# Joining a sequence's query-row transfers in the second attention of a two-layer kernel

## The reference

```
x = x + L0_attn(layernorm(x))          # linear attention, 16 heads of 8
x = x + L0_ffn(layernorm(x))           # 8 experts, each takes its top 129 tokens
x = x + L1_attn(layernorm(x))          # changed here
x = x + L1_ffn(layernorm(x))           # fft, product, inverse fft

def L1_attn(x):                        # x: 8 x 512 x 128, HEAD_D = 8, 16 heads
    qkv = x @ w_attn                   # 128 columns of q, 8 of k, 8 of v
    q = qkv[..., :D].reshape(Bv, Tv, H, HEAD_D).transpose(0, 2, 1, 3)
    k, v = qkv[..., D:D + HEAD_D], qkv[..., D + HEAD_D:]
    att = einsum('bhqd,bkd->bhqk', q, k) / sqrt(8), causal
    y = einsum('bhqk,bkd->bhqd', softmax(att), v)
    return y @ w_proj
```

## Time and profile before

| | us |
|---|---|
| median of three timed runs (lowest, highest) | 917.9 (916.76, 918.37) |
| the profiled execution's own time | 917.51 |
| its span, first to last instruction | 915.8 |
| start of the second attention's first query transfer | 442.60 |
| first scores of turn 0 | 500.40 |
| first scores of turn 1 | 548.09 |

### The profile page before, as it was taken

How to read it: one execution, slowest core, us unless ns; L and a number is a source line. 1 busy time by engine, 2 the same in 40 slices (tenths; PEclk the granted TensorE clock), 3 DMA queues, 4 the chain that set the end, 5 groups by cost and what they waited for, 6 DMA issues and landing times.

```text
span 915.8 us, 15035 instructions
## 1 busy us (share of the span) xinstructions
PE 689.0 (75%) x4377; PEld 413.0 (45%) x4409; DVE 578.8 (63%) x1934; ACT 336.8 (37%) x614; POOL 336.3 (37%) x438
## 2 busy tenths in 40 slices
PE   2788998860399999992553878888787878788866
PEld 1455665540178877771220324343433334243325
DVE  8388888869323344436474776858585868768126
ACT  1422322125032232320301646555455545455642
POOL 0475555610578667740000222222222222223324
PEclk9999999985599999995555999979898989989898
DMA  9100000005122222231011010101000000000003
GB/s 296 58 1 1 1 0 0 1 1 149 34 45 41 38 38 44 39 50 34 29 42 37 14 33 15 36 16 37 19 31 26 23 32 15 32 13 1 3 1 92
DMA packets 41861, 32.43 MB, mean 35 GB/s; under 512 B 5120, under 2 KB 38448, under 8 KB 41792
## 3 DMA queue, kind: packets, MB, share of 16 engines
q1 hardware_dynamic: 32608, 24.10, 8.5%
q0 software_dynamic: 7840, 6.86, 5.0%
q10 hardware_dynamic: 1344, 0.62, 0.3%
HBM read 13.60 MB, written 8.13 MB: 24 GB/s over the span
## 4 chain that ended last, share of the span: by engine, by line
PE 21%; DVE 13%; issue 9%; SPq 6%; ACT 2%; DMA 2%; POOL 1%; DVEq 0%; POOLq 0%; ACTq 0%
PE bank L1665 5%; PE wide L1652 5%; DVE masked L1321 5%; SPq L1543 5%; PE bank L1604 5%; PE bank L1677 2%; DMA qT<-mT 2%; ACT pexp L1475 2%; DVE mx L1321 2%; DVE st L286 1%; SPq L1549 1%; PE bank L1689 1%; PE bank L1579 1%; DVE q_rest L1279 1%; PE bank L1586 1%
## 5 line engine op out<-in xcount | busy, mean ns | idle before, releaser
L1321 DVE CUSTOM_DVE_ANT_0 masked<-bank,mask_qk 128x128 f32<-128x128 f32 (+2 forms) x496 | 216.6, 487 | 60.7 <-PE bank L1604 58.9
L1427 POOL TENSOR_SCALAR_AFFINE_SELECT pexp<-pexp 128x256 f32<-128x256 f32 x256 | 103.0, 407 | 363.6 <-ACT pexp L1475 360.6
L1475 ACT ACTIVATE pexp<-wide 128x1024 f32<-128x1024 f32 (+3 forms) x256 | 168.6, 707 | 161.8 <-PE wide L1652 161.0
L1604 PE MATMUL bank<-kTm,qT 128*128 128x128 bf16 (+3 forms) x474 | 117.0, 314 | 29.2 <-DVE mx L1321 23.8
L1652 PE MATMUL wide<-qT,kTe 128*128 128x256 bf16 (+3 forms) x503 | 113.3, 325 | 32.9 <-DMA qT<-mT 23.8
L1604 PEld LDWEIGHTS bank<-kTm,qT 128*128 128x128 bf16 x496 | 44.2, 101 | 129.9 <-DVE mx L1321 100.5
L1665 PE MATMUL bank<-pexp,vx 128*32 128x512 f32 (+3 forms) x1024 | 96.6, 450 | 2.2 <-POOL pexp L1427 1.1
L1068 ACT ACTIVATE hT<-wide,b1T 128x512 f32<-128x512 f32 x64 | 44.0, 688 | 137.0 <-PE wide L1088 137.0
L935 POOL DMA_INDIRECT x_row<-xln_dram,row_u x64 | 63.4, 990 | 52.8 <-DVE slot_tok L813 33.6
L1652 PEld LDWEIGHTS wide<-qT,kTe 128*128 128x128 bf16 x512 | 46.0, 102 | 76.2 <-ACT pexp L1475 27.1
L942 POOL DMA_INDIRECT x_dram<-yg,row_u x40 | 63.8, 1595 | 31.1 <-DVE yg L991 21.1
(11 more groups left out here) (226 smaller groups left out, 1039.8 us busy)
## 6 DMA issues: line engine op xcount, KB each, us to landing
qT<-qp SPq DMA_DIRECT2D x288, 32.0 KB
x_sb<-in_L_attn_x SPq DMA_DIRECT2D x8, 256.0 KB, 6.9
w_sb<-in_L_ffn_w SPq DMA_DIRECT2D x1, 2048.0 KB, 12.4
xln_dram<-rx SPq DMA_DIRECT2D x8, 256.0 KB, 2.3
out_x<-x_sb SPq DMA_DIRECT2D x8, 256.0 KB, 2.3
x_dram<-x_sb SPq DMA_DIRECT2D x5, 256.0 KB, 3.5
x_sb<-x_dram SPq DMA_DIRECT2D x5, 256.0 KB, 2.8
x_row<-xln_dram,row_u POOLq DMA_INDIRECT x64, 2.6
```

The costliest lines, as they stand in the source:

```text
L1321: ins = nc.vector.tensor_tensor_reduce(out=masked[:, n % 4, at], in0=bank_of(n)[:, at], in1=mask_qk[:, T - w:T], scale=1.0, scalar=LEAST, ...
L1427: nc.gpsimd.affine_select(out=pexp[:, n % 4, :, 0:P], in_=pexp[:, n % 4, :, 0:P], pattern=[[0, 2], [1, P]], compare_op=ALU.is_ge, fill=0.0 ...
L1475: nc.scalar.activation(pexp[:, n % 4, :, 0:w], psE[n % 2][:, :].rearrange("p (h t) -> p h t", h=2)[:, :, 0:w], ACT.Exp, scale=SCALE).then_ ...
L1604: ins = nc.tensor.matmul(place[:, hh * w:(hh + 1) * w], qT[:, b % 2, h + hh, k * P:(k + 1) * P], kTm[:, b % 2, 0:w], start=True, stop=True)
```

## The change

A sequence's query rows come in nine transfers of 128 KB, one for each pair of query part and key part: from all 128 partitions of `qp` into 8 partitions of `qT`, with all 16 heads. To that end `wq2` orders the columns as (feature, head). `qT` gets a third buffer (`QB = 3`), which lengthens the MEMSET of partitions 64 to 127 by half. The four semaphores of the quads become one, so each maximum waits for all nine transfers. SyncE issues sequence b + 2 whole in turn b, once the scores of sequence b - 1 are done. The shift rows are one transfer of 48 KB from 48 partitions into 3.

```
-        qT = sb("qT", [P, 2, HEADS, T], BF16)
+        qT = sb("qT", [P, QB, HEADS, T], BF16)
...
-        q_row = [Q(f"q_rows_of_quad_{qd}", PARTS * PARTS, 16) for qd in range(NQ)]
+        q_row = Q("q_rows", PARTS * PARTS, 16)
...
-        q_mTp, q_mT, q_mrow = Q("neg_max_T_psum"), Q("neg_max_T"), Q("shift_rows", PARTS, 16)
+        q_mTp, q_mT, q_mrow = Q("neg_max_T_psum"), Q("neg_max_T"), Q("shift_rows", 1, 16)
...
-            nc.vector.tensor_copy(wq2[:, :].rearrange("p (q l h) -> p q l h", l=L, h=4),
-                                  wa_sb[:, 0:D].rearrange("p (q h l) -> p q l h", h=4, l=L)).then_inc(q_init.sem, 1)
+            nc.vector.tensor_copy(wq2[:, :].rearrange("p (l h) -> p l h", l=L),
+                                  wa_sb[:, 0:D].rearrange("p (h l) -> p l h", l=L)).then_inc(q_init.sem, 1)
...
-            for qd in range(NQ):
-                act.wait_ge(q_row[qd].sem, q_row[qd].at(b, 0))
+            act.wait_ge(q_row.sem, q_row.at(b, 0))
...
-        def sp_q_rows(sp, b, quads):
-
-            for qd in quads:
-                if b >= 2:
-                    sp.wait_ge(q_sp.sem, q_sp.at(b - 2, 2 * NT * (qd + 1)))
-                for n in range(PARTS):
-                    sp.wait_ge(q_qpart.sem, q_qpart.at(b, 2 * n + 1))
-                    for j in range(PARTS):
-                        row = (n * PARTS + j) * L
-                        sp.dma_start(qT[row:row + L, b % 2, 4 * qd:4 * qd + 4, :],
-                                     qp[32 * qd:32 * qd + 32, n, :]).then_inc(q_row[qd].sem, 16)
+        def sp_q_rows(sp, b):
+
+            if b >= QB:
+                sp.wait_ge(q_sp.sem, q_sp.at(b - QB, NX))
+            for n in range(PARTS):
+                sp.wait_ge(q_qpart.sem, q_qpart.at(b, 2 * n + 1))
+                for j in range(PARTS):
+                    row = (n * PARTS + j) * L
+                    sp.dma_start(qT[row:row + L, b % QB, :, :], qp[:, n, :]).then_inc(q_row.sem, 16)
 
         def sp_shift_rows(sp, b):
             sp.wait_ge(q_mT.sem, q_mT.at(b, 1))
-            for n in range(PARTS):
-                sp.dma_start(qT[QR + n:QR + n + 1, b % 2, :, :],
-                             mT[n * HEADS:(n + 1) * HEADS, :]).then_inc(q_mrow.sem, 16)
+            sp.dma_start(qT[QR:QR + PARTS, b % QB, :, :], mT[:, :]).then_inc(q_mrow.sem, 16)
...
-                sp_q_rows(sp, b, range(NQ))
+                sp_q_rows(sp, b)
             sp_shift_rows(sp, 0)
             for b in range(B - 1):
-                if b:
-                    sp_q_rows(sp, b + 1, (NQ - 1,))
                 if b + 2 < B:
-                    sp_q_rows(sp, b + 2, range(NQ - 1))
+                    sp_q_rows(sp, b + 2)
                 sp_shift_rows(sp, b + 1)
...
-            pe.wait_ge(q_row[h // 4].sem, q_row[h // 4].at(b, PARTS * PARTS))
+            pe.wait_ge(q_row.sem, q_row.at(b, PARTS * PARTS))
```

More of the change, by code:

```diff
@@ L61, in build @@
     NQ = HEADS // 4
+    QB = 3
     with ExitStack() as ctx:
@@ L1603, in pe_max_unit @@
             for hh in range(nh):
-                ins = nc.tensor.matmul(place[:, hh * w:(hh + 1) * w], qT[:, b % 2, h + hh, k * P:(k + 1) * P],
+                ins = nc.tensor.matmul(place[:, hh * w:(hh + 1) * w], qT[:, b % QB, h + hh, k * P:(k + 1) * P],
                                        kTm[:, b % 2, 0:w], start=True, stop=True)
@@ L1643, in pe_scores @@
             if step == 0:
-                pe.wait_ge(q_mrow.sem, q_mrow.at(b, PARTS))
+                pe.wait_ge(q_mrow.sem, q_mrow.at(b, 1))
                 pe.wait_ge(q_kTe.sem, q_kTe.at(b, 1))
@@ L1651, in pe_scores @@
                     at = psE[half][:, hh * 512:hh * 512 + w]
-                    ins = nc.tensor.matmul(at, kTe[:, par, j * P:(j + 1) * P], qT[:, par, h, j * P:T],
+                    ins = nc.tensor.matmul(at, kTe[:, par, j * P:(j + 1) * P], qT[:, b % QB, h, j * P:T],
                                            start=True, stop=True)
```

## The result

The changed kernel takes 927.34 us in the median of four runs (925.35 to 927.5), the kernel before 917.88 on the same footing: a ratio of 1.010, interval 1.0082 to 1.0117. It is slower by 9.5 us where I had forecast 4.7 (922.2 against 917.5), and 1.3 us above my range. A second comparison on another chip gave 925.67 and a ratio of 1.0082 (1.006 to 1.0104), so the size is 8.3 to 9.5 us. The profiled execution took 925.35, the shortest of the four, with a span of 923.6, 7.8 us more than the 915.8 of before; what follows is read from it.

What follows compares the result with a forecast made beforehand. SyncE's queue of query-row issues was taken to delay the second attention's first scores, its shift issues each later turn; neighbouring partitions limit writes. 917.5 + 3.4 (clearing) + 1.3 (start), turns 0, gave 922.2 us, range 911 to 926.

Steps and rivals of the forecast that it cites:

- The start of the second attention: From first query issue to scores: nine slower landings, partly made up by sequence 1's parts following at once; +1.3 us.
- Period 2.2 us: Query transfers at the second attention's start: each 128 KB takes 2.2 us, chosen between 2.0 and 2.4.
- parts of sequence 1 with no pause: Second attention's start: qp is long free after two quads, so sequence 1's parts begin at once.
- 4.3 us to the next maximum: Second attention's start: maxima resume 4.3 us after sequence 1's parts begin, at 482.5, 7.4 late.
- SyncE free when mT is ready: Second attention's start: SyncE's queue is free, so the shift transfer starts at 498.3, when mT is ready.
- Clearing: Kernel's start: VectorE's clearing of qT's upper half grows by half, with no cover; +3.4 us, bounds +3.2 to +3.5.
- Shift rows and turns: Shift wait in each later turn: 3.4 us from issue to landing against 3.39 before, so no change.
- 7 x 0: Seven later turns: the two issues saved (1.2 us) go into the longer write of shift rows, adding nothing.
- My upper bound for it, +0.4 a turn: Joined shift transfer in a turn: all 48 packets on one engine, 3.8 us to landing, +0.4 a turn.
- C: Query and shift transfers: no write limit, scores start 11.2 us earlier, turns win 4.0; 905.7 us, or 910; chance 0.15.
- B: Query transfers: writes of successive transfers overlap well, period 1.2 to 1.9; 915.9 us (913 to 919); chance 0.15.
- D: Query transfers: period from 2.5 on, shift rows stand behind sequence 1's rows; 927.6 us at 2.8; chance 0.10.

Runs made afterwards that it cites:

- e4: Changed kernel with contraction rows reordered so each 128 KB transfer writes eight partitions nine apart instead of eight neighbours: 914.8 us, ratio 0.9968.
- e12: Kernel before, still with 32 KB query transfers, but with the contraction rows in the spread order: 919.5 us, ratio 1.0015.
- e1: Kernel before with a third query buffer allocated and cleared but never used: 921.5 us, ratio 1.0043.
- e2: Kernel before with the shift rows joined into one 48 KB transfer into three neighbouring partitions: 920.9 us, ratio 1.0037.
- e3: Changed kernel with the shift rows in three transfers of 16 KB again: 922.89 us, ratio 1.0051.
- e9: e5 with the third query buffer cleared by VectorE ahead of the second attention's first maxima instead of at the kernel's start: 899.15 us, ratio 0.9803.
- e5: Changed kernel with query rows spread as in e4 and the joined shift transfer onto partitions 72, 76 and 80: 903.49 us, ratio 0.9848.
- e7: e5 with all three query buffers cleared by GpSimd instead of VectorE: 908.21 us.

## Why the prediction was wrong

- **The start of the second attention: right.** Period 2.2 us, ninth landing 21.5 us after the first issue; measured 20.8, so a period of 2.1. To the first scores I had +1.3 us, measured +0.85; two small errors offset each other in part, since mT was ready 0.9 us earlier than in my sum and the shift rows took 0.4 longer. Each step of it (parts of sequence 1 with no pause, 4.3 us to the next maximum, SyncE free when mT is ready) stands in the trace. e4 shows that the cause is the one I gave, the destination's neighbourhood, and e12 that it was hidden at 32 KB.
- **Clearing: right in kind, 0.85 us short.** 3.42 is what the instruction grew by; it also starts 0.85 later, in every kernel with three buffers cleared in the start (3.97 or 3.98 for 3.12). e1 measures 4.2. What makes it start later I did not find out; that cause stays open.
- **Shift rows and turns: the failed step.** The term "7 x 0" of my sum was mis-sized; it measured 3.0 us in the profile (turns 0 to 6) and 3 to 4.5 in the runs. The landing came 3.60 instead of 3.4 us after the issue. I put it down to the longer issue (0.76 for 0.58), which I had left out: the first byte passes about 1.4 us after the issue, where I had 1.25. That is 0.2 a turn. And I assumed that a turn grows by what its wait grows by, when the earlier trace rows show waits only, not what the granted clock does after them. e2 puts the term at +3.6, e3 at 3 to 4.5. My upper bound for it, +0.4 a turn, holds about that much, but I did not carry it into the range. With the terms as measured (clearing 4.2, start 0.85, turns 3.0 to 3.6) the sum gives 8 to 8.7 us in place of my 4.7.
- **Rivals.** C (no write limit) falls with e4; so does B, whose periods of 1.2 to 1.9 would have needed the writes to overlap more than 2.1 shows. D gave nearly the measured time (927.6) by luck, for a wrong reason: the rows of sequence 1 had long landed when mT was ready. The third buffer removed no wait in a turn, as I had it.
- The joining pays after all once the destinations lie apart, which no case of mine contained: e9 is 18.2 us faster than the kernel before.

## What to carry to other kernels

Before you join transfers, look at what a single one does after its last byte has passed the DMA engines: if the landing comes late, as here by 0.6 us for 16 KB and for 32 KB, the destination may be the limit, and a larger transfer shows it in full. Spread the destination partitions (here nine apart, by another order of the contraction rows) and the same bytes can go faster, here 2.6 times. How large a group of neighbours shares the limit was not measured here: the runs compare eight neighbours with eight partitions nine apart, and three neighbours with three that are four apart. And price a wait of TensorE by the turns of several kernels, not by its own length, since the clock after it may add to it or swallow it.

## What the runs showed of the hardware that I had not expected

- Issues do not get dearer with size here: 0.61 us for 128 KB in 128 packets, 0.67 for 32 KB in 32, but 0.76 for 48 KB into three partitions against 0.58 for 16 KB into one.
- Three engines for three destination rows: the window of one joined shift transfer has 51 packets, three of them small, and yet e5's landing is 0.7 us better than three transfers over sixteen engines:

```profile
DMA packets 51, 0.05 MB, mean 10 GB/s; under 512 B 3, under 2 KB 51, under 8 KB 51
```

- Eight neighbouring partitions took 63 GB/s over nine transfers, more than the 54 that single transfers suggested. That fits with writes of successive transfers, which go to other partitions, overlapping a little; no run tests it.
- GpSimd's clearing is half as fast as VectorE's, and two small VectorE instructions beside it, the one that takes 0.18 us before and the cast behind it, end only when it ends (10.94 us in e7), while the batch statistics do not get slower.
